# Score maxima of five heads instead of four reduced in the following step, in a fused attention and mixture-of-experts kernel

## The reference

```
x = x + layernorm(attention(layernorm(x)))        # 16 heads of 16, BigBird-like block mask, 8 blocks of 64
x = x + layernorm(ffn(layernorm(x)))              # dense branch + 8 experts, top 2, 3 rotations, gate
# attention, for each head: q, k, v = x W + b; p = softmax(q k^T / 4 over the blocks allowed); p v
```

## Times and profile before

| | us |
|---|---|
| median of 3 runs | 1788.7 (1787.45 to 1792.31) |
| the profiled execution | 1799.32 |
| its span (first to last instruction) | 1797.5 |
| PE busy over the span | 1543.8 |
| DVE / ACT / POOL busy | 1228.8 / 898.9 / 705.7 |

### The profile page before, as it was taken

How to read it: one execution, slowest core, us unless ns; L and a number is a source line. 1 busy time by engine, 2 the same in 40 slices (tenths; PEclk the granted TensorE clock), 3 DMA queues, 4 the chain that set the end, 5 groups by cost and what they waited for, 6 DMA issues and landing times. The chain is left out here.

```text
span 1797.5 us, 33500 instructions
## 1 busy us (share of the span) xinstructions
PE 1543.8 (86%) x10385; PEld 1062.6 (59%) x10386; DVE 1228.8 (68%) x3690; ACT 898.9 (50%) x1789; POOL 705.7 (39%) x716
## 2 busy tenths in 40 slices
PE   7889999999999999999999888399999999999500
PEld 5645555545554555455545556288888888888400
DVE  5667787788787878787888633356565665555287
ACT  3146766676667666766776553033333333333244
POOL 1011323442444335333542244144444444544377
PEclk9999999999999999999999989699999999999855
DMA  8132245335533543354334127645656656564397
GB/s 229 36 119 79 88 138 170 119 108 172 160 119 111 177 153 116 123 174 142 123 120 162 52 95 230 191 96 117 134 125 126 134 114 143 105 147 78 48 321 229
DMA packets 186637, 243.59 MB, mean 136 GB/s; under 512 B 23624, under 2 KB 157136, under 8 KB 186384
## 3 DMA queue, kind: packets, MB, share of 16 engines
q1 hardware_dynamic: 159632, 205.67, 36.5%
q0 software_dynamic: 26880, 36.33, 12.4%
HBM read 133.40 MB, written 105.91 MB: 133 GB/s over the span
## 5 line engine op out<-in xcount | busy, mean ns | idle before, releaser
L1053 ACT ACTIVATE pexp<-scT 128x512 f32<-128x512 f32 x768 | 433.6, 598 | 258.7 <-PE scT L839 256.1
L1240 DVE TENSOR_REDUCE mx<-work 128x1 f32<-128x320 f32 (+2 forms) x1024 | 500.6, 547 | 64.3 <-PE work L812 63.7
L1747 POOL DMA_INDIRECT y_rows<-rows_add,row_of x144 | 227.5, 1580 | 298.6 <-DMA y_rows<-rows_add,row_of 235.1
L839 PE MATMUL scT<-w 128*128 128x192 bf16 (+3 forms) x1536 | 282.1, 275 | 26.6 <-ACT pexp L1053 21.8
L812 PE MATMUL work<-w 126*128 126x320 bf16 (+4 forms) x1280 | 269.6, 295 | 31.0 <-DVE mx L1240 27.4
L1779 PE MATMUL h_ps<-inT,w1c 128*128 128x256 f32 x1152 | 263.5, 382 | 2.4 <-DVE inT L1831 2.4
L1792 PE MATMUL o_ps<-w,hT 128*128 x1152 | 260.4, 379 | 0.0
L1722 ACT ACTIVATE rows_add<-rows_out,row_share 128x257 f32<-128x257 f32 x144 | 65.6, 503 | 355.1 <-DVE rows_out L1847 266.3
L1779 PEld LDWEIGHTS h_ps<-inT,w1c 128*128 128x128 f32 x1152 | 220.7, 192 | 33.6 <-issue 3.2
L1792 PEld LDWEIGHTS o_ps<-w,hT 128*128 128x128 f32 x1152 | 213.4, 190 | 26.1
L839 PEld LDWEIGHTS scT<-w 128*128 128x128 bf16 x1536 | 123.5, 97 | 177.6 <-ACT pexp L1053 128.7
(11 more groups left out here) (191 smaller groups left out, 2086.8 us busy)
## 6 DMA issues: line engine op xcount, KB each, us to landing
w<-split_spill SPq DMA_DIRECT2D x384, 128.0 KB, 2.9
split_spill<-split SPq DMA_DIRECT2D x64, 384.0 KB, 3.2
rows_in<-z_rows SPq DMA_DIRECT2D x72, 265.0 KB, 4.8
y_rows<-pre SPq DMA_DIRECT2D x16, 514.0 KB, 5.7
y<-y_rows SPq DMA_DIRECT2D x16, 514.0 KB, 6.7
x_rows<-x SPq DMA_DIRECT2D x16, 512.0 KB, 2.9
abel_rows<-pre SPq DMA_DIRECT2D x16, 512.0 KB, 3.6
abel_in<-abel_rows SPq DMA_DIRECT2D x16, 512.0 KB, 4.4
```

Source lines behind the costliest of these rows:

```text
L839: ins = nc.tensor.matmul(scT[n % 2][:, at:at + hi - lo], tile(kst[par][0:K_EXP, h, :], t), qst[par][0:K_EXP, h, lo:hi], start=True, stop=True)
L1053: nc.scalar.activation(pexp[:, (q * GROUP + n) % NPB, :], scT[n % 2][:, :], ACT.Exp, scale=DH ** -0.5).then_inc(s_exp, 1)
L1240: emptied(nc.vector.reduce_max(mx[:, c:c + 1], bank(s, "max", b, h, t)[:, 0:n], AX_X), s, "max", b, h, t)
L1747: pool.indirect_dma_start(kept.y_rows, bass.IndirectOffsetOnAxis(ap=row_of[n][:, r:r + 1], axis=0), rows_add[n % 2][:, r, :], None, comput ...
```

## The change

Five heads are late instead of four (EARLY is 11), so 20 units have a place in `LATE_AT` instead of 16. The four units at the end of quad 11 are now those of head 11 (before, of head 12). Three units of head 12 stand ahead of the first projection of the next step ("before"), the fourth and the first of head 13 behind projection 0; the other three of head 13 behind projections 1 to 3, and heads 14 and 15 in the quads, as before. On DVE all five stand ahead of the first projection's `parts`. The early part has 44 columns instead of 48, the late part 20 instead of 16.

```
-EARLY = 12
+EARLY = 11
 LATE_TURN_AT = 3
 LATE_AT = [("end", 1), ("end", 2), ("end", 3), ("end", 3),
-           ("proj", 0), ("proj", 1), ("proj", 2), ("proj", 3),
+           ("before",), ("before",), ("before",), ("proj", 0), ("proj", 0), ("proj", 1), ("proj", 2), ("proj", 3),
            ("quad", 0, 3), ("quad", 0, 3), ("quad", 1, 3), ("quad", 1, 3), ("quad", 1, 3),
            ("quad", 2, 1), ("quad", 2, 2), ("quad", 2, 3)]
@@ order_of
+            if here(s, 1):
+                maxima(s - 1, late("before"))
             for m in range(4):
                 if here(s, 0):
                     seq.append(("project", m))
@@ reduced
-            units = [(h, t) for h in ((11,), (15,))[part] for t in range(NT)]
+            units = [((EARLY, HEADS)[part] - 1, t) for t in range(NT)]
@@ step of TensorE
+                if attend:
+                    for h, t in late("before"):
+                        max_unit(s, s - 1, 1 - par, h, t)
                 for m in range(4):
                     if proj:
                         project(s, m)
@@ step of DVE
+                behind("before")
+                behind("proj", 0)
                 for m in range(4):
                     if proj:
                         parts(s, m)
                     if finish and m % 2:
                         finish_a(s - 2, m // 2)
-                    behind("proj", m)
+                    if m:
+                        behind("proj", m)
```

## The result

The changed kernel takes 1838.8 us (median of 6 runs, 1836.5 to 1845.2), against 1791.6 us for the kernel before on the same occasion (6 runs, 1787.5 to 1793.4). The ratio is 1.0275, with a 95% interval of 1.0254 to 1.0295: some 49 us slower by the ratio, 47 by the medians. The profiled execution took 1838.76 us, 39.4 us more than that of before (1799.32), which had been a long one.

The account below looks back on a forecast made before the run. TensorE was taken to set the pace. Wait 44.2 + shift 4.5 - given back 15.6 and 2 + clock 9 = 40 us, so the median goes from 1788.7 to about 1829, own range 1810 to 1845 (chance 0.70).

Parts of the forecast that it names:

- The wait: TensorE at quad 6 waits for the late heads' rows, 3.0 to 4.6 us in ten steps, 44.2 us in all.
- The units around the first projection: Four more units there cost nothing in themselves, covered by VectorE's idle 4.25 us ahead of the first `parts`.
- The shift of SP's queue: SP's queue, starting from the splits, moves 0.3 us a step (0 to 0.9), 4.5 us over 15 steps.
- What is given back: Behind the wait 1.3 us return in eleven steps, 15.6 us in all; 2 us more in two steps without it.
- The clock: TensorE's clock falls behind the new waits part of the time: 0.8 us in eleven steps, 9 us.
- the rival that the clock falls in every step: TensorE's clock falls in every step with a long wait, 28 us instead of 9: 1848; chance 0.22.
- The sum: All terms add 40 us to the profiled execution, 1799.3 to 1839; the median goes to about 1829.
- Swallowed: TensorE's existing gaps in a step absorb the wait, leaving 6 us, 1795, counted as no change; chance 0.04.
- Faster: Rows arrive by quad 6, moved units fill VectorE's idle time: 1.4 us in 15 steps, 21 us, 1768; chance 0.04.
- The landing: Late rows' second DMA takes 4.4 to 5.4 us in steps with stores; 2 us everywhere would give about 1803.

Follow-up runs that it names:

- e1: The changed kernel with SP putting the late heads' rows ahead of the load of x for batch s-2 and the two big stores: 1784.0 us, ratio 0.9956.
- e3: The kernel before with TensorE's wait for the late rows at quad 6 instead of quad 9, no unit moved: 1845.3 us, ratio 1.0287.
- e5: The kernel before with head 12's units moved around the first projection, still four late heads and the wait at quad 9: 1790.5 us, ratio 1.0001.
- e4: The changed kernel with 12 extra score products on TensorE ahead of the late rows' wait in eleven steps: 1826.8 us, ratio 1.0206.
- e6: The kernel before with TensorE's wait for the late rows at quad 7 instead of quad 9, nothing else: 1791.2 us, ratio 1.0009.
- e7: The changed kernel with SP putting the late rows right ahead of the two big stores, behind both loads of x: 1789.1 us, ratio 0.9990.

## Why the prediction was right, and where its terms were off

- **The wait.** It stands where it was forecast, at quad 6, for the late rows, 4.1 us in the step shown, and e1 and e3 show it to be the whole cause. From TensorE's last product to the weight load of the first score, its sum is 52.8 us in 14 waits (the 57.6 of the page reach to the second score), above the 40 to 50 that I named. One of them, 1.6 us, is in step 1, where I had expected none. For the rest, TensorE comes to quad 6 about 0.8 us earlier in the step (e1, where it does not wait there, shows this alone), a term that I had rightly counted as worth nothing there and then left out of the length of the wait. The landing is where it was, 29.5 us behind the first exponential of the step and 29.7 before. What the wait adds to the time is how much later in the step the first score of quad 6 starts: 42.8 us over the thirteen steps of my sum, where I had 44.2 + 4.5 for wait and shift, 6 us too much.
- **The units around the first projection.** They cost nothing (e5), and their cover is as worked out, 1.8 us of VectorE's gap being left where I had 1.5. The shift of SP's queue, set at 0.3 us a step, was 0.1: the second DMA is issued 25.4 us behind the step's first exponential, 25.3 before. It then took 4.1 us to land in the mean, 4.4 before.
- **What is given back.** From the first exponential of quad 6 to the first of the next step it took 33.7 us before and takes 33.4 us after, where the clock stays up. ScalarE's rows of two steps of the changed kernel, each quad 6 and the next step's start:

```profile
512.94 0.60 ACT L1058 ACTIVATE pexp<-scT 128x512 f32<-128x512 f32 x1 [2.77 <-remote]
```

```profile
546.35 1.08 ACT L1058 ACTIVATE pexp<-scT 128x512 f32<-128x512 f32 x2
```

```profile
576.34 0.60 ACT L1058 ACTIVATE pexp<-scT 128x512 f32<-128x512 f32 x1 [3.53 <-remote]
```

```profile
611.01 1.08 ACT L1058 ACTIVATE pexp<-scT 128x512 f32<-128x512 f32 x2
```

  That is 546.35 - 512.94 = 33.4 without a fall of the clock. The weights of the first score of that step are loaded at 512.51, so ScalarE is 512.94 - 512.51 = 0.43 us behind it, and was 0.96. The give-back is 0.3 + 0.5, about 0.9 us a step, against my 1.3. In e3, where no unit is moved, the steps without a fall give back 0.55 us: the backlog that I had at 0.5 was right, and the two units and the maximum, which I had at 0.8, are worth 0.3.
- **The clock.** This is the term that was too small. In the second pair of rows it is 611.01 - 575.69 = 35.3 us from the weight load of the first score, with one fall of 3.4 us, against 546.35 - 512.51 = 33.8 in the first: 1.5 us more. Over the steps a fall of 3.4 us costs 1.1 to 1.5 us and one of 6.8 us costs 1.8 us; there were ten in steps 2 to 13, some 15 us, where I had 9. e4 gives 12 with three falls left, which cost some 4. I had shared the chance between my forecast and the rival that the clock falls in every step. It fell in nearly every step, as the rival has it, but a fall cost 1.5 us in the mean and not the rival's 2.5. That ScalarE, which bounds quads 6 and 7, hides the difference is likely, but no run separates it. The Trainium skill's picture ("TensorE: Matmul & The Clock Gate", HAM oscillation) of a clock lost again in each round of a loop that waits for a DMA is borne out here, in ten of the eleven steps with a wait of over 3 us.
- **The sum.** For each step of the stretch: 3.5 us by which quad 6 starts later, 0.9 given back and 1.4 of clock are 4.0 us; from the first exponential of step 4 to that of step 13 the mean period went from 60.7 to 64.7 us, 4.0 more. I had 3.75 + 0.3 - 1.3 + 0.8 = 3.55. Over all steps, 42.8 of wait, 15 of clock and the rest, some 14 given back, make the 44 us by which the last exponential of `front` moves in the profiled executions, from 1064.4 to 1108.4; I had 48.7 + 9 - 17.6 = 40. So the mechanism was right, but the sum came nearer than its terms, because their errors cancel in part: that is luck. What comes after `front`, which the change doesn't touch, was 4.5 us shorter in the execution of after; hence 39.4. The medians differ by 47. The forecast of 1829 was 10 us low: 3 us because the median of before was 1791.6 with more runs, 4 us from the terms, and 3 us that I did not settle.
- **The rivals.** "Swallowed" fell: e6 shows that a wait under 1 us is, and e3 that one of 3.6 us is not. "Faster" was right on its condition (with the rows there in time the kernel is faster, e1) and wrong in its price: 8 us, not 21. e5 shows one reason: a gap of TensorE taken away in front of ScalarE's exponentials opens again there.
- **The landing.** With the fixed cost of about 2 us that the Trainium skill states ("DMA: Bandwidth & Descriptors", Latency and other measured facts) I had estimated 1803. The measurement decides against 2 us for rows issued behind the stores (4.1 us in the mean after, 4.4 before) and for it once they are ahead (e7, 1.9 us).

## What to carry to other kernels

When a number that splits work in two is changed, look for every wait that is computed from it: here `EARLY // GROUP * NCH` was in no line of the diff and moved a wait by three quads. Take the landing of the transfer from the trace (issue plus its own time behind the traffic before it) and subtract the time at which the waiting engine will come; a difference under the slack that follows is free (e6), and one beyond it counts, less what comes back behind the wait (0.9 us a step here) and, on TensorE, with the clock's falls on top (1.4 us a step here). A small transfer that someone waits for belongs ahead of the large stores in the queue, for which nobody waits.

## What the runs showed of the hardware that was not expected

The length of a wait on TensorE did not decide by itself whether the clock fell behind it. In the changed kernel the waits of over 3 us are 3.3 to 5.0 us long. Behind this one of 3.6 us (the row reaches to the second score)

```profile
512.74 0.38 PE L841 MATMUL scT<-w 128*128 128x512 bf16 x1 [3.81 <-DMA w<-mrow]
```

the clock stayed at its upper level; behind the next, of 4.1 us, it was at half for 3.4 us, and behind the shortest, of 3.3 us in step 12, too. In other steps it was at half for 6.8 us. In step 2 of e1 a wait of 2.4 us was enough, where the record is complete; the second row is the stretch behind it, at 0.50:

```profile
190.89 0.60 PE L843 MATMUL scT<-w 128*128 128x512 bf16 x2 [2.40 <-DMA w<-mrow]
```

```profile
192.40:195.60 3.20, 3.20 (x25) 1.37 (x14) 1.80 (x5) 2.74 (x7) 0.94 (x2) 0.50 0.32 97
```

Filling 2.75 us of each wait with products (e4) left 1.8 us of idling and took most of the falls away, though not all. The unused products cost nothing that can be seen.

SP's issue of the two rows took 1.67 us (e1, e7) with nothing large ahead, 1.2 us in an early step of before with 16 instead of 20 rows in each, and 2.4 us behind the stores, so part of the lateness is in the issue itself.
